# Twelve one-hot tables instead of five, z in four chunks, the last tile's gathers held back

## The reference

```python
e = stack([tbl_0[ids[:, 0]], ..., tbl_25[ids[:, 25]]], axis=1)      # 512 x 26 x 128
combined = concatenate([dense[:, None, :], e], axis=1)               # 512 x 27 x 128
inter = einsum('bfd,bgd->bfg', combined, combined)[:, iu, ju]        # 351 pairs f < g
h = concatenate([dense, inter, dense], axis=1)                       # 512 x 607
h = relu(h @ W_top1 + b_top1)                                        # 512 x 512
h = relu(h @ W_top2 + b_top2)                                        # 512 x 256
y = h @ W_top3                                                       # 512 x 1
```

## Time and profile before

| what | value |
|---|---|
| device time, median of 3 runs | 226.74 us (223.83 to 226.93) |
| span of the profiled execution, first to last instruction | 152.9 us |
| that execution's own device time | not recorded |
| busy: PE, DVE, ACT, POOL | 115.3, 51.1, 49.8, 83.9 us |
| mean granted TensorE clock, share of 2.4 GHz | 0.866 |
| moved by DMA | 12.82 MB |

### The profile page before, as it was taken

One profiled execution on the slowest core, in us unless ns is written; L12 is line 12 of the kernel. 1 busy time (PEld: TensorE's weight loads), 2 busy tenths in 40 slices (PEclk: granted clock), 3 DMA queues, 4 the chain that ended last, 5 costly groups with the idle time before them and its releaser, 6 DMA issues.

```text
span 152.9 us, 3980 instructions
## 1 busy us (share of the span) xinstructions
PE 115.3 (75%) x1789; PEld 95.1 (62%) x1789; DVE 51.1 (33%) x88; ACT 49.8 (33%) x98; POOL 83.9 (55%) x91
## 2 busy tenths in 40 slices
PE   0339401999379965599899899958999949995993
PEld 0127201677157654486788788647989739994691
DVE  6665600076457810712103800234500405104100
ACT  5045203368499840703000800204500106104011
POOL 4777777777787877777777777777710000000000
PEclk9999955569978999557999999997799996999659
DMA  1684447999644322221222221122210000000000
GB/s 43 151 192 164 166 164 227 270 248 238 172 166 167 119 53 57 50 57 51 55 53 56 58 51 51 51 56 56 60 30 0 0 9 0 4 4 0 4 0 1
DMA packets 5547, 12.82 MB, mean 84 GB/s; under 512 B 2025, under 2 KB 3049, under 8 KB 5277
## 3 DMA queue, kind: packets, MB, share of 16 engines
q0 software_dynamic: 2688, 5.51, 15.2%
q1 hardware_dynamic: 2832, 7.05, 15.0%
q10 hardware_dynamic: 10, 0.01, 0.0%
HBM read 12.56 MB, written 0.00 MB: 82 GB/s over the span
## 4 chain that ended last, share of the span: by engine, by line
PE 57%; DMA 25%; DVE 7%; issue 7%; ACT 2%; SPq 1%; ACTq 0%
DMA table_sb<-tbl 25%; PE h_ps L539 17%; PE gram_ps L511 9%; PE h_ps L563 7%; PE h_ps L534 6%; PE fill_ps L485 5%; DVE zT L391 5%; PE gram_ps L462 3%; PE gram_ps L539 3%; PE gram_ps L464 3%; DVE featT L385 2%; ACT featT L301 1%; PE gram_ps L534 1%; PE h_ps L573 1%; DVE h L396 1%
## 5 line engine op out<-in xcount | busy, mean ns | idle before, releaser
L289 POOL DMA_INDIRECT gathered<-tbl,ids_sb x84 | 83.1, 989 | 26.9 <-issue 25.3
L539 PE MATMUL h_ps<-zT,w_inter_sb 122*128 122x128 f32 (+1 forms) x196 | 29.2, 295 | 1.6 <-DVE zT L391 1.6
L539 PEld LDWEIGHTS h_ps<-zT,w_inter_sb 122*128 122x128 f32 (+1 forms) x196 | 27.3, 203 | 4.7 <-DVE zT L391 1.9
L462 PE MATMUL gram_ps<-onehot,table_hi 125*128 125x512 f32 x40 | 20.8, 519 | 4.8 <-DVE table_lo L424 4.7
L314 ACT ACTIVATE zT<-gram_ps 26x224 f32<-26x224 f32 (+4 forms) x40 | 12.1, 302 | 37.7 <-PE gram_ps L511 36.9
L418 DVE TENSOR_TENSOR onehot<-h_ps,rowno 125x1536 fp32r<-125x1536 f32 x10 | 17.5, 1755 | 17.8 <-PE gram_ps L464 16.9
L511 PE MATMUL gram_ps<-featT 128*26 128x26 f32 (+2 forms) x1280 | 15.5, 188 | 9.0 <-issue 5.8
L391 DVE COPY zT<-gram_ps 26x224 f32<-26x224 f32 (+4 forms) x40 | 12.9, 323 | 24.6 <-PE gram_ps L511 23.5
L511 PEld LDWEIGHTS gram_ps<-featT 128*26 128x26 f32 (+1 forms) x1280 | 13.2, 102 | 11.9 <-issue 7.5
L464 PE MATMUL gram_ps<-onehot,table_lo 125*128 125x512 f32 x40 | 19.6, 490 | 0.0
L307 ACT ACTIVATE featT<-fill_ps 128x512 f32<-128x512 f32 (+1 forms) x14 | 9.1, 656 | 26.4 <-PE fill_ps L485 26.4
(11 more groups left out here) (33 smaller groups left out, 55.5 us busy)
## 6 DMA issues: line engine op xcount, KB each, us to landing
table_sb<-tbl SPq DMA_DIRECT2D x5, 500.0 KB
w_inter_sb<-w_inter SPq DMA_DIRECT2D x1, 1792.0 KB, 29.9
gathered<-tbl,ids_sb POOLq DMA_INDIRECT x84, 3.8
oh_ids_sb<-oh_ids SPq DMA_DIRECT2D x1, 1000.0 KB
w_dense_sb<-w_dense SPq DMA_DIRECT2D x1, 512.0 KB, 25.0
w_sb<-w SPq DMA_DIRECT2D x1, 512.0 KB, 26.8
dense_sb<-dense SPq DMA_DIRECT2D x1, 256.0 KB, 23.2
oh_ids_sb<-oh_ids SPq DMA_DIRECT2D x1, 250.0 KB
```

What stands on the lines that cost most here:

```text
L289: pool.indirect_dma_start(out=gathered[:, t, pos - GATHERED[0], :], out_offset=None, in_=tables[table], in_offset=bass.IndirectOffsetOnAxi ...
L462: nc.tensor.matmul(lookup_ps(k), table_hi[:, k % 2, rows], onehot[:, c, :], start=(c == 0), stop=False)
L539: last = nc.tensor.matmul(layer1_ps(t, n), w_inter_sb[0:k, c, units], zT[0:k, c, tile], start=False, stop=(c == CHUNKS - 1), skip_group_ch ...
```

## The change

Twelve tables, all those of 1000 rows, go by lookup, and 14 by gather. Tables are padded to 1024 rows, 128 partitions of 8. The ids of a lookup are in SBUF for both DVE and ACT: a transfer of its own spreads them for each table (only table 0's come by a matmul). DVE compares chunk by chunk, 6 or 7 of 8 chunks; ACT makes the other 2 or 1 with one closing instruction. There are three buffers for raw tables, split tables and ids, two for the one-hot matrix, and PSUM results are copied in pairs. featT has rows of 32 slots: 27 features and five copies. With these, products are 32 x 27, and zT has four chunks of 128 full rows; each of the 16 strips is written by two instructions, an upper part over a lower one (CUT, ABOVE, BELOW). The dense part of layer 1 reads its own tile denseT. The last tile is one stage. POOL has three row buffers and starts the last tile's 14 gathers only when gram_ready has reached 2.

```diff
-ONEHOT_TABLES = (0, 1, 3, 6, 8)
+ONEHOT_TABLES = (0, 1, 3, 6, 8, 11, 12, 14, 15, 16, 18, 20)
-RPARTS = ROWS // RCHUNKS
+PADDED = P * RCHUNKS
...
+ZCHUNKS = 4
+CUT = (3, 9, 16, 22)
...
+def dve_chunks(k):
+    return 6 + k % 2
...
-            sp.dma_start(oh_ids_sb[:, 1:, :], oh_ids[1:].partition_broadcast(RPARTS)).then_inc(oh_ids_in[1], 16)
+            def spread_ids(k):
+                if k >= IDS_BUFS:
+                    sp.wait_ge(id_off_ready, act_chunks_to(k - IDS_BUFS + 1))
+                    sp.wait_ge(onehot_dve, dve_chunks_to(k - IDS_BUFS + 1))
+                sp.dma_start(ids_all[:, k % IDS_BUFS, :], oh_ids[k].partition_broadcast(P)) \
+                    .then_inc(ids_all_in[k % IDS_BUFS], 16)
...
             for t in range(TILES):
+                if t >= ROW_BUFS:
+                    for bank in range(2):
+                        pool.wait_ge(filled[bank], fills_of_bank(bank, fill_no(t - ROW_BUFS, len(GROUPS) - 1) + 1))
+                if t == LAST:
+                    pool.wait_ge(gram_ready, LAST - 1)
...
-                    nc.vector.tensor_tensor(onehot[:, c:c + DVE_STEP, :],
-                                            oh_ids_ps(k).unsqueeze(1).to_broadcast(of_step),
-                                            rowno[:, c:c + DVE_STEP].unsqueeze(2).to_broadcast(of_step),
-                                            ALU.is_equal).then_inc(onehot_dve, DVE_STEP)
+                nc.vector.tensor_scalar(onehot[:, k % 2, c, :], ids_all[:, k % IDS_BUFS, :], rowno[:, c:c + 1], None,
+                                        ALU.is_equal).then_inc(onehot_dve, 1)
...
+                for q in range(4):
+                    nc.vector.tensor_copy(z_target(t, j, q, QUAD), z_source(t, j, BELOW[q], QUAD)).then_inc(z_dve, 1)
+                for q in range(4):
+                    dve.wait_ge(z_dve, ZCOPIES * (2 * t + half) + q + 1)
+                    nc.vector.tensor_copy(z_target(t, j, q, CUT[q]), z_source(t, j, ABOVE[q], CUT[q])).then_inc(z_dve, 1)
...
-                        last = nc.tensor.matmul(
-                            gram_ps[stage % 2][QUAD * j:QUAD * j + rows, col + first:col + rows],
-                            featT[:, b, 0:rows], featT[:, b, 1 + first:1 + rows], start=True, stop=True)
+                        last = nc.tensor.matmul(product_ps(t)[QUAD * j:QUAD * (j + 1), SLOTS * s:SLOTS * s + FEATS],
+                                                featT[:, b, :], featT[:, b, 0:FEATS], start=True, stop=True)
```

More of the change, by code:

```diff
@@ L62 @@
[L62 to L93, removed]
@@ L96, in tower @@
-def tower(nc, dense, ids, oh_ids, tables, w_inter, w_dense, b1, w2, b2, w3, out):
+PADDED = P * RCHUNKS
+FIRST = PADDED // P // 2 * DIM
+RAW_BUFS = 3
+ROW_BUFS = 3
+SPLIT_BUFS = 3
+IDS_BUFS = 3
+SLOTS = 32
+DENSE_SLOT = 2
+PAIR_SLOTS = ((4, 7), (9, 10), (0, 1), (3, 5), (6, 8), (11, 12))
+COPIED = (2, 4, 7, 9, 10)
+FIRST_GATHERED = 1 + ONEHOTS
+GROUP = 4
+GROUPS = [range(p, min(p + GROUP, FEATS)) for p in range(FIRST_GATHERED, FEATS, GROUP)]
+FIELD_AT = {DENSE_SLOT: 0}
+FIELD_AT.update(zip([slot for pair in PAIR_SLOTS for slot in pair], [1 + n for n in ONEHOT_TABLES]))
@@ L97, in tower, with act_chunks_to, quads @@
+def act_chunks_to(k):
+    return RCHUNKS * k - dve_chunks_to(k)
+def quads(cols):
+    a, b, c, d = cols
+    if a + d == b + c:
+        return a, c - a, b - a
+    raise ValueError(cols)
+def tower(nc, dense, ids, oh_ids, tables, w_inter, w_dense, small, w2, out):
     fp32, fp32r, i32 = mybir.dt.float32, mybir.dt.float32r, mybir.dt.int32
@@ L193, in dve_reads @@
         def dve_reads(t, g):
-            return fill_no(t, g) % 2 == 0 and not transposed_early(t, g)
+            return t >= 2 and fill_no(t, g) % 2 == 0
         def fills_of_bank(bank, upto):
@@ L434, in _ @@
[L434 to L444 removed]
+            dve.wait_ge(small_in, 16)
@@ L527, in layer1 @@
[L527 to L541 removed]
+                    pe.wait_ge(denseT_ready, 1)
@@ L542, in layer1 @@
                     last.then_inc(h1_psum, 1)
-            def layer1_before(stage):
-                layer1_start(stage)
-                for n in range(N1 - BESIDE[stage]):
-                    layer1(stage, n)
+                elif n == N1 - 1:
+                    last.then_inc(h1_psum_last, 1)
             def layer2(t):
@@ L552, in layer2, with layer2_last @@
                     pe.wait_ge(w2_in, 16)
-                if t > 0:
-                    pe.wait_ge(y_ready, t)
+                pe.wait_ge(h1_ready, N1 * (t + 1))
+                for n in range(N2):
+                    for k in range(N1):
+                        last = nc.tensor.matmul(layer2_ps(t, n), w2_sb[:, k, n * P:(n + 1) * P],
+                                                h1[:, t % 2, k, :], start=(n == 0 and k == 0), stop=(k == N1 - 1),
+                                                skip_group_check=True)
+                last.then_inc(h2_psum, 1)
+            def layer2_last():
+                pe.wait_ge(h2_ready, N2 * LAST)
                 for half in range(2):
-                    if half == 0 or t < LAST:
-                        pe.wait_ge(h1_ready, N1 * t + (half + 1) * N1 // 2)
+                    if half == 0:
+                        pe.wait_ge(h1_ready, N1 * LAST + N1 // 2)
                     else:
@@ L608, in _ @@
-            layer3(LAST - 1)
-            layer1_start(len(STAGES) - 1)
+                for t, g in AFTER_LOOKUP[k]:
+                    fill(t, g)
+            layer1_dense(0)
+            products(0, 0)
+            products(0, 1)
+            layer1_dense(1)
+            products(0, 2)
+            products(0, 3)
+            fill(2, 0)
+            products(1, 0)
+            products(1, 1)
+            fill(2, 1)
+            products(1, 2)
+            products(1, 3)
+            fill(2, 2)
@@ new lines, in _ @@
+            layer1(0, 0)
+            layer1(0, 1)
+            fill(2, 3)
+            layer1(0, 2)
+            products(2, 0)
+            products(2, 1)
+            layer1(0, 3)
+            products(2, 2)
+            products(2, 3)
+            layer1(1, 0)
+            layer1(1, 1)
+            layer2(0)
+            layer1(1, 2)
+            layer1(1, 3)
+            layer1_dense(2)
+            layer1(2, 0)
+            fill(3, 0)
+            layer1(2, 1)
+            layer1(2, 2)
+            fill(3, 1)
```

615 lines of the change are left out of this document (342 added, 273 removed).

## The result

The changed kernel took **145.88 us** (median of 4 runs, 145.38 to 148.33), the kernel before 225.63 on the same chip (223.83 to 226.93): a ratio of 0.645, 95% interval 0.640 to 0.650. The forecast was 202 us, its range 193 to 222. The direction was right, the size was not: 80 us were saved where 25 were forecast.

The account below looks back on a forecast made before the run. Lookups waiting for table loads bound the kernel up to 54 us, PE after. Lookups +13 us and the rest -38 cut the span by 25, and 226.74 - 25 gives 202 us, range 193 to 222.

Parts of the forecast that it names:

- The sum's base: Whole kernel: span falls from 152.9 to 128 us, and that 25 is taken off the measured median of 226.74.
- the forecast's own -25: Whole span: lookups 67 us for 54 (+13), the rest 61 for 99 (-38), so 25 us less.
- Loads: Table loads before the lookups: 12.7 MB at 233 GB/s, 55 us, so tables barely no longer end the wait.
- Start of the products at 67 us, by ACT: End of lookups: ACT's 60 us of work from about 5 us on lets products begin at 67 us.
- Compares: One-hot compares on DVE in the lookups: 78 at about 0.44 us, 52 us with low parts; rival rate 0.69, 71 us.
- DVE and POOL: Lookups: rival that DVE becomes the bound, by slow compares or mutual hold-up with POOL; 209 to 222 us, chance 0.19.
- The strong lock: Lookups: rival that gathers also stop DVE, up to 0.95 us for each of 42; 226 to 236 us, chance 0.07.
- the weak one: Lookups: only gathers stretch beside DVE, to 2.3 us each; 211 us, part of the DVE-bound rival, chance 0.19.
- Lower clock: PE: rival that bursts keep it at 1.2 GHz, lookups 6.9 us each; 245 us, chance 0.09 with anything like it.
- After the lookups: Products, z copies, layers and tail after the last lookup: 61 us for 99, z 5.0 a tile, layer-1 blocks 1.25.
- E: The end of the last lookup, from which the second part is laid out; forecast at 67 us.
- Held gathers: Last tile's 14 gathers: landed by 32 us after the lookups, wanted at 37, hidden; rival that they bite, chance 0.05.

Follow-up runs that it names:

- a_nohold: Changed kernel without POOL's wait before the last tile's 14 gathers, on a 153-chip: 124.9 us, ratio 0.811 to the kernel before.
- a_pace05: Changed kernel with a 128x512 zero fill on POOL after each gather of tiles 2 and 3, on a 153-chip: 124.41 us, ratio 0.814.
- a_hold3: Changed kernel with the last 14 gathers held one tile longer, until the products of tile 2, on a 153-chip: 127.52 us, ratio 0.824.
- b_pad128: Kernel before with its five one-hot tables padded to 1024 rows, 128 partitions instead of 125, on a 153-chip: 142.09 us against 153.26.
- a_nohold2: Changed kernel without POOL's wait before the last tile's 14 gathers, on a 226-chip: 151.96 us, ratio 0.671 to the kernel before.
- b_same2: Kernel before, unchanged, run again for its trace on a 226-chip: 226.03 us.

## Why the prediction failed

**The sum's base is the step that failed**: "The durations come from one execution whose own time is not known; its difference is put on the median". That took 73.8 us as lying outside the span and unchanged. 1.8 us lie outside; 72 were starving, inside a span that the profile shown did not have. Most of it went: 73 us are lost to it before (226.03 - 152.88), some 20 after (145.9 against 124 to 128 for its neighbours a_nohold, a_pace05 and a_hold3 on 153-chips; the changed kernel itself had no run there). PE's wait for issue in the products agrees: 24.4 us here, 6.7 to 7.1 in those three. That is 53 of the 80 us.

The other 27 are the forecast's own -25. On 153-chips the neighbours have spans of 123.1, 124.4 and 126.3 us, where 128 was forecast. That this is so near is in part luck: the lookups were put 8 us too long and what follows them 4 us too short. By its steps:

- **Loads**: right that they no longer bound the lookups. Up to 58 us the core moved 237 GB/s at a share of 0.73, and the chain has 1% DMA. The 233 GB/s taken as the bound were no bound (370 in b_pad128), which cost the forecast nothing.
- **Start of the products at 67 us, by ACT**: it was 59.1, and PE was the bound (51.5 us busy of 58; the lookups' matmuls are 33% of the chain). ACT was busy 50.3 us where I had 60: pair copies cost 1.47 and 1.14, not 1.9 (9.6 for 13.3), and ACT's instructions overlap by 0.1 us or more where I had added gaps of 0.05 (60 times). 8 us too late.
- **Compares**: 0.43 each, 48.4 us on DVE for 52. Right.
- **DVE and POOL**: gathers did stretch (1193 ns mean for 989 in the earlier trace rows), compares did not. The strong lock is refuted, and the weak one cost no time in the lookups.
- **Lower clock**: 1.00 up to 58 us. Refuted there; afterwards it was 0.69 and 0.52 on average in the two starved stretches, in which PE is mostly idle.
- **After the lookups**: 61 us from E; in a_nohold 64.6 (123.1 - 58.5). The z of tile 0 began there at 67.8, 9.3 us behind E and not 5.4: two stalls of 2.42 and 1.11 us in the products, where the 5.4 has none and one of 1.8 was only called possible. The z copies were 0.28 each and 5.0 us a tile, as forecast; the tail 15.6 for 17.3. A block of layer 1 was 1.11 for 1.25: the chain of the changed kernel has the dense parts of four blocks (8 instructions), then one block's four matmuls.

```profile
116.17 0.89 PE h_ps L594 x8
117.06 0.89 PE h_ps L604 x8
```

- **Held gathers**: hidden, as said. That the hold could gain something was not in the argument at all. With spaced gathers on one 153-chip it is worth nothing (124.41 and 124.11); with unspaced ones on a 226-chip 6 us.

The range failed for the same reason: it was built from the costs of engines around a base that no row supported.

## What to carry to other kernels

If span and measured time differ by more than a few us, find out why before forecasting: here a 74 us gap held the largest effect of the change. Gathers by index on GpSimd are not free when off the critical path; on some chips they hold up PE, DVE and ACT, so issue fewer of them, or leave about 0.5 us between them. On the other chips that costs nothing where the gathers have slack (the changed kernel) and 9 us where they do not (the kernel before). The spaced version, 138.9 and 124.4 us, is the best that was run on both kinds.

## What the hardware showed that was not expected

- Two kinds of chips: 226 and 153 us for one kernel (seven chips, four and three), with the same DMA rate (170 and 171 GB/s from 34 to 54 us) and the same duration of a gather (0.98 us on average), and a ratio of the change of 0.645 on the first and about 0.81 (neighbours) on the second.
- On a 226-chip, beside gathers in an unbroken row, one per 1.25 us, PE got 1 to 6 products every 0.7 to 2 us, and DVE waited up to 38.9 us. The stall outlived the last gather: by 1.8 us in the changed kernel, 4.2 in a_nohold2 and over 10 in b_same2. 84 plain loads of the same size by the same engine did nothing like it.
- The recorded durations of successive instructions of ACT and DVE overlap: 0.43 us per compare for a recorded 0.49.
- Table loads over 128 partitions, with gathers beside them, moved 370 GB/s for 11 us, over 125 partitions 162.
